# Batch loop of a fused attention kernel: shift additions and exponentials in one operation each, odd steps' exponentials last on ScalarE

## The reference, cut to what matters

```python
def xattn(q, k, v, ...):                       # 16 batch items, 16 heads of 32, 128 queries, 2048 keys
    qh = (q @ wq + bq) ; kh = (k @ wk + bk) ; vh = (v @ wv + bv)     # split into heads
    attn = einsum('bhqd,bhkd->bhqk', qh, kh) / sqrt(32)
    score = softmax(attn, axis=-1)
    return einsum('bhqk,bhkd->bhqd', score, vh) @ wo + bo
x = x + xattn(layernorm(x), ctx, ctx, ...)     # the batch loop is in here
x = x + linear_attention_block(layernorm(x))   # with its own MLP
x = x + fp4_ffn(layernorm(x))
```

## Time and profile before

| | us |
|---|---|
| median of the runs | 3409.68 (3409.34 to 3410.42, 3 runs) |
| the profiled execution, its own time | 3413.08 |
| its span, first to last instruction | 3411.3 |
| busy in the span: PE, PEld, DVE, ACT, POOL | 3351.7, 2675.1, 2422.9, 1361.7, 2144.2 |
| mean granted TensorE clock | 0.998 of full speed |
| additions of the shift (L1377) | 480, 582.2 us busy |
| exponentials (L1229) | 480, 509.2 us busy |

### The profile page before, as it was taken

How to read it: one execution, slowest core, us unless ns; L and a number is a source line. 1 busy time by engine, 2 the same in 40 slices (tenths; PEclk the granted TensorE clock), 3 DMA queues, 4 the chain that set the end, 5 groups by cost and what they waited for, 6 DMA issues and landing times.

```text
span 3411.3 us, 82033 instructions
## 1 busy us (share of the span) xinstructions
PE 3351.7 (98%) x32279; PEld 2675.1 (78%) x32279; DVE 2422.9 (71%) x3740; ACT 1361.7 (40%) x1970; POOL 2144.2 (63%) x1564
## 2 busy tenths in 40 slices
PE   8999999999999999999999999999999999999999
PEld 6777777777777777777777777778777788878887
DVE  6566766666666666676666766666776688789997
ACT  2244454444554445444444445444223322321111
POOL 3277978879788797797987978863555400023332
PEclk9999999999999999999999999999999999999999
DMA  4111111111111111111111111122222423410000
GB/s 150 58 36 36 40 37 45 39 37 40 35 45 39 35 39 38 45 39 35 41 36 44 39 36 45 39 78 74 84 78 86 131 93 103 129 65 19 25 18 19
DMA packets 201799, 183.21 MB, mean 54 GB/s; under 512 B 10272, under 2 KB 167072, under 8 KB 199840
## 3 DMA queue, kind: packets, MB, share of 16 engines
q1 hardware_dynamic: 201504, 178.64, 16.6%
HBM read 140.59 MB, written 38.01 MB: 52 GB/s over the span
## 4 chain that ended last, share of the span: by engine, by line
PE 92%; DVE 5%; issue 1%; DMA 1%; ACT 0%; POOL 0%; SPq 0%; DVEq 0%; POOLq 0%; ACTq 0%
PE a_bank L100 67%; PE a_bank L1567 6%; PE a_bank L1576 6%; PE a_bank L1609 6%; PE a_bank L711 1%; PE a_bank L2608 1%; PE a_bank L1554 1%; DVE x_probsT L1377 0%; PE a_bank L1582 0%; PE a_bank L722 0%; PE a_bank L1628 0%; DVE x_maxima L1366 0%; PE a_bank L1597 0%; PE a_bank L776 0%; PE a_bank L780 0%
## 5 line engine op out<-in xcount | busy, mean ns | idle before, releaser
L1366 DVE TENSOR_REDUCE x_maxima<-a_bank 128x1 f32<-128x512 f32 x960 | 615.5, 682 | 356.2 <-PE a_bank L1567 356.2
L1229 ACT ACTIVATE x_probsT<-x_probsT 128x1024 f32<-128x1024 f32 x480 | 509.2, 1061 | 813.1 <-DVE x_probsT L1377 813.1
L100 PE MATMUL a_bank<-x_ctx,x_wk 128*128 128x512 f32 x3072 | 775.8, 401 | 0.0
L100 PE MATMUL a_bank<-x_wv,x_ctx 128*128 128x512 f32 x3072 | 744.4, 391 | 0.0
L100 PEld LDWEIGHTS a_bank<-x_ctx,x_wk 128*128 128x128 f32 x3072 | 558.7, 188 | 158.9 <-issue 21.0
L100 PEld LDWEIGHTS a_bank<-x_wv,x_ctx 128*128 128x128 f32 x3072 | 573.2, 188 | 130.4 <-ACT x_v L1211 5.4
L948 POOL TENSOR_TENSOR x_pairs<-x_probsT 128x1024 f32<-128x1024 f32 x240 | 576.4, 2402 | 13.0 <-ACT x_probsT L1229 10.8
L1377 DVE TENSOR_TENSOR x_probsT<-a_bank,x_shift_all 128x1024 f32<-128x1024 f32 x480 | 582.2, 1213 | 3.1 <-PE a_bank L1576 3.0
L1122 POOL TENSOR_TENSOR x_ctx<-x_tile_raw,x_one 128x512 fp32r<-128x512 f32 x236 | 245.3, 1039 | 332.4 <-PE a_bank L100 331.3
L1403 DVE SCALAR_TENSOR_TENSOR x_k<-a_bank,x_bk,x_k 128x512 fp32r<-128x512 f32 x240 | 180.2, 751 | 303.8 <-ACT x_k L1218 303.8
L1124 POOL TENSOR_TENSOR x_ctx<-x_tile_raw,x_ctx 128x512 fp32r<-128x512 f32 x236 | 301.4, 1277 | 18.5
(11 more groups left out here) (218 smaller groups left out, 4429.7 us busy)
## 6 DMA issues: line engine op xcount, KB each, us to landing
x_tile_raw<-in_ctx SPq DMA_DIRECT2D x236, 256.0 KB, 3.1
m_ff_src<-in_w_ff SPq DMA_DIRECT2D x44, 192.0 KB, 2.5
wq_ff<-m_ff_dst SPq DMA_DIRECT2D x44, 192.0 KB, 1.8
attT<-x_out SPq DMA_DIRECT2D x32, 256.0 KB, 2.0
s_attT<-attT SPq DMA_DIRECT2D x16, 512.0 KB, 3.9
m_w_raw<-in_w SPq DMA_DIRECT2D x32, 256.0 KB, 2.9
f_w_in<-wq_ff SPq DMA_DIRECT2D x22, 256.0 KB, 3.2
x_ctx_raw<-in_ctx SPq DMA_DIRECT2D x5, 1024.0 KB, 5.3
```

The lines of the kernel that those rows point to most:

```text
L100: mm = pe.matmul(out, lhs[a], rhs[b], start=first and n == 0, stop=last and n == 2)
L1229: act.activation(half, half, ACT.Exp).then_inc(exped, 1)
L1366: dve.tensor_reduce(maxima[:, c, g * HG + j:g * HG + j + 1], banks[:, j], AX.X, ALU.max).then_inc(maxed, 1)
```

## The change

Each step's two additions of the shift (heads 0 and 1, then 2 and 3) become one addition over all four heads, and it stands where the first half stood: between the maxima of heads 0 and 1 and those of heads 2 and 3. The step's two exponentials become one over all four heads. In even steps it takes the place of the first (in step 0 behind the copy `query_hi`), in odd steps it stands at the end of ScalarE's list, behind `values`. Both semaphores still count two for each step, so `values` on TensorE now waits for the whole addition. What is computed is the same. The work goes from 480 additions and 480 exponentials of 128x1024 to 240 of each of 128x2048.

```diff
-            def exp(i, s, h):
-                act.wait_ge(shifted, START + i * (2 * NS) + (2 * s + h + 1))
-                half = probs(i, s)[:, 2 * h:2 * h + 2].rearrange("p j t s -> p (j t s)")
-                act.activation(half, half, ACT.Exp).then_inc(exped, 1)
+            def exp(i, s):
+                act.wait_ge(shifted, START + i * (2 * NS) + (2 * s + 2))
+                whole = probs(i, s)[:].rearrange("p j t s -> p (j t s)")
+                act.activation(whole, whole, ACT.Exp).then_inc(exped, 2)
...
             def even_step(i, s, past, follow):
-                exp(i, s, 0)
                 if s == 0:
                     query_hi(i + 1)
+                exp(i, s)
+                if s == 0:
                     copy_spread(i, 1)
-                exp(i, s, 1)
                 keys(i, s)
...
             def odd_step(i, s, follow):
-                exp(i, s, 0)
                 keys(i, s)
                 if s == 1:
                     copy_spread(i, 2)
                 if s == NS - 1 and follow:
                     copy_spread(i + 1, 0)
-                exp(i, s, 1)
                 values(i, s)
+                exp(i, s)
...
-            def add_shift(i, s, h):
-                if h == 0:
-                    dve.wait_ge(scored, START + i * NS + (s + 1))
-                    await_count(dve, pv_done, i * NS + (s - 3))
-                    await_count(dve, paired, i * NS + (s - 3))
-                    if s < DC:
-                        dve.wait_ge(shift_kept, START + kept_at(i, SHIFT_KEPT[s]))
-                two = slice(2 * h, 2 * h + 2)
-                dve.tensor_tensor(probs(i, s)[:, two], scores[:, two].rearrange("p j (t s) -> p j t s", t=TPC),
-                                  shift_all[s % DC][:, two].rearrange("p j (o s) -> p j o s", o=1)
-                                  .to_broadcast([P, 2, TPC, S]), ALU.add).then_inc(shifted, 1)
+            def add_shift(i, s):
+                dve.wait_ge(scored, START + i * NS + (s + 1))
+                await_count(dve, pv_done, i * NS + (s - 3))
+                await_count(dve, paired, i * NS + (s - 3))
+                if s < DC:
+                    dve.wait_ge(shift_kept, START + kept_at(i, SHIFT_KEPT[s]))
+                dve.tensor_tensor(probs(i, s)[:], scores.rearrange("p j (t s) -> p j t s", t=TPC),
+                                  shift_all[s % DC][:].rearrange("p j (o s) -> p j o s", o=1)
+                                  .to_broadcast([P, HG, TPC, S]), ALU.add).then_inc(shifted, 2)
...
-                add_shift(i, s, 0)
+                add_shift(i, s)
                 if top:
                     maximum_by_head(*top, tops, (2, 3))
-                add_shift(i, s, 1)
...
             def values(i, s, amid=None):
-                pe.wait_ge(shifted, START + i * (2 * NS) + (2 * s + 1))
+                pe.wait_ge(shifted, START + i * (2 * NS) + (2 * s + 2))
```

## The result

| | before | after |
|---|---|---|
| median of the runs, us | 3409.51 (3406.24 to 3410.42, 4 runs) | 3466.86 (3465.24 to 3469.02, 4 runs) |
| ratio, 95% interval | | 1.017 (1.0153 to 1.0188) |
| span of the profiled execution | 3411.3 | 3464.2 |

The account below looks back on a forecast made before the run. TensorE was taken as the bound; new waits of 30.9 + 14.9 + 10.9 + 2.7 + 0.7 = 60.1 us on the profiled 3413.1 gave 3473.2, and 3469.8 us as median, 1.8% slower. The range was 3452 to 3490 us.

Parts of the forecast that it names:

- The bound: Whole kernel: TensorE, busy 98%, bounds it; savings on VectorE or ScalarE are worth nothing by themselves.
- the first rival: Whole loop: fewer instructions make it faster, VectorE saving 0.145 us in each of 240 steps, 34.8 us; 3%.
- The size of the operations: VectorE and ScalarE: a whole addition takes 2.28 us, a whole exponential 1.91 us.
- Steps 15 and 1: Spreads there wait for maxima of heads 2 and 3, 1.067 us later, at 29 places: 30.9 us.
- full in every slice: TensorE's granted clock, read as full throughout the profile, was taken to stay so at cost 0.
- Step 2: Denominators wait for the maximum of head 2, 1.067 us later in 14 items: 14.9 us.
- Step 0: Spread amid the keys: 0.78 us of new wait for the maxima in 14 items, 10.9 us.
- The absorbed case: Rival: waits behind step 0 absorb its 10.9 us and odd steps cost nothing, 3452 to 3456 us; 12%.
- Plain odd steps: Values' load waits for the whole addition; about 0.03 us reaches the matmuls in 90 steps, 2.7 us.
- Exponentials last: Odd steps' exponentials end 0.1 us before the next step's second `weigh` needs them: cost 0 in 120 even steps.
- 0.7 us for the two `weigh`: After the loop's last item, the two `weigh` follow without scores between and wait once: 0.7 us.

Follow-up runs that it names:

- the later exponential: The changed kernel with one more ScalarE copy of 128x128 ahead of each odd step's exponential; 3469.24 us.
- ScalarE's part alone: The kernel before with whole exponentials, those of odd steps last, and additions still in halves; 3464.14 us, ratio 1.0159.
- e_dve_only: The kernel before with whole additions, its exponentials still in halves at their old places; 3478.22 us, ratio 1.0203.
- e_mix2: Against the changed kernel: exponentials last, additions whole in even steps and halved in odd, four maxima ahead in even steps, 1 and 15; 3401.89 us.
- e_best: e_mix2 with steps 1 and 15 on VectorE as in the kernel before, and their spreads in the middle of the values; 3391.52 us, ratio 0.9945.

## Why the prediction was right

**The bound.** TensorE's own work sets the loop's pace and VectorE's saving was worth nothing: VectorE was busy 9.3 us less and ScalarE 38.5 less, and the time rose. The 34.8 us that the first rival counted for VectorE were too many in any case: the additions alone fell by 34.2 us (582.2 to 548.0), but VectorE's operations overlap by some 0.08 us, and with 240 of them gone some 19 us of overlap (an estimate) are gone too.

**The size of the operations.** Whole addition 2.281 us against 2.279 taken from the SBUF row, whole exponential 1.906 against 1.91. The formula of the Trainium skill, "VectorE: DVE Perf Modes", section on the TRN2 errata, gives 2.29, and the trace agrees. Its advice of larger tiles held for the engine (0.14 us saved for a pair) and not for the kernel.

**Steps 15 and 1.** 1.067 us each was forecast, 1.06 and 1.11 measured. The count was one too many, 28 places and not 29, so 1 us. In step 1 of the first item the changed kernel's spread does wait (its weight load 1.30 us, its matmul 0.90), but the step is 0.10 us shorter. The two kernels' keys and spread there:

```profile
179.70 4.34 PE L100 MATMUL a_bank<-x_ctx,x_wk 128*128 128x512 f32 x12
183.88 0.40 PE L1582 MATMUL a_bank<-x_shift_rows,x_pick 128*128 128x512 f32 x1
```
```profile
179.09 3.27 PE L100 MATMUL a_bank<-x_ctx,x_wk 128*128 128x512 f32 x12
183.26 0.47 PE L1578 MATMUL a_bank<-x_shift_rows,x_pick 128*128 128x512 f32 x1 [0.90 <-issue]
```

Before, TensorE did most of its keys at a granted clock of 0.50 (175.7 to 182.6); in the changed kernel that stretch began at 176.2 and ended at 179.6. The clock gave back what the wait took. That is luck, and the forecast's "full in every slice" was read from slices of 85 us, which don't show such a stretch.

**Step 2.** 1.067 forecast, 1.05 measured, in 14 items.

**Step 0.** 0.78 forecast, 0.71 measured. The absorbed case is out: nothing behind it gave this back. Moving the spread three matmuls later removed it.

**Plain odd steps.** 2.7 us forecast, some 2 measured, unevenly. Step 3 has the most (0.09): its whole addition starts 2.31 us after the first load of `top`, where in the other odd steps it starts at 2.23, and the values' load comes at 4.66. In steps 5, 11 and 13 the load comes at 4.57 for 4.49 and the step grows by 0.03; in steps 7 and 9 it was at 4.53 already and nothing is lost.

**Exponentials last.** Forecast at no cost with 0.1 us of cover. Right for the changed kernel, by its waits and by the later exponential, but I gave the reason half: "Even steps' exponentials end earlier than before, and nobody waits for them". TensorE does want them, two engines on: the copies of the keys stand behind the even steps' exponential. That it ends in time there rests on the other part of the change, and a kernel with ScalarE's part alone loses 53 us. The forecast costed the two parts as a sum; they aren't one. Its 0.7 us for the two `weigh` after the last item measured nothing: they start 1.77 us after the first load of the last `top` in both kernels, and 1.86 us in a plain even step, so they are 0.1 us early there and not the estimated 0.8.

**What is left.** The loop grew by 56.5 us, the profiled span by 52.9. Of the 3.6 us between, 0.5 lie ahead of the loop and 3.2 behind it, where the change has nothing. Behind it the kernel before has two stretches of 3.4 us at a granted clock of 0.50 (from 3022.5 and from 3056.6), the changed one has one (from 2698.7). Held against each other matmul by matmul, the two kernels move by 1.6 us at each of the three, so 1.6 of the 3.2 us are the clock's. I have no cause for the rest.

## What to carry to other kernels

Merging two operations of an engine that isn't the bound saves that engine a little (0.14 us for a pair here), and delays everything that used to be released by the first half and everything that stood between the halves: list who waits for each of those, and compare the delay with how far ahead the release came. Follow it through a second engine too, as an operation made longer delays those behind it on its own queue. Where a wait does appear, moving the waiting instruction behind a few independent ones on the bound engine can give back all of it and more.

## What the runs showed of the hardware

- A weight load may be late without the matmuls being late: 0.10 us late at the load cost 0.02 to 0.04 us in the step, and in the plain odd steps 0.07 us late cost about 0.03.
- After a release TensorE's load came 0.05 us later where one wait remained (1400.48 to 1400.53), and 0.2 to 0.4 us later where several stood in a row (1414.82 to 1415.03, 1402.90 to 1403.30). That it is their number, and not something else about these places, wasn't tested by itself.
- The page's 40 slices can hide a fall of TensorE's clock, and it isn't the same in each kernel. In step 1 of the first item, behind a stand of TensorE of 3.25 us, the granted clock was 0.50 for 6.8 us in the kernel before, for 3.4 us in the changed one and not at all in e_dve_only; behind a stand of 1.9 us it was 0.50 for 3.4 us in e_mix2 and stayed full in e_best. Behind the loop each stretch of 3.4 us at 0.50 cost 1.6 us.
